# The fourth layer's support made tile by tile during the third layer, and its epilogue taken off TensorE

## What is computed

```python
h = relu(layernorm(x)); x = x + L0(h, adj, ...)      # graph attention, elu
h = relu(layernorm(x)); x = x + L1(h, adj, W, b)     # normalized adj @ h @ W + b, relu
h = relu(layernorm(x)); x = x + L2(h, adj, weight)   # adj @ (sign(h) @ sign(weight).T), relu
h = relu(layernorm(x)); x = x + L3(h, adj, t, weight)

def L3(x, adj, t, weight):
    ts = t[0]
    support = x @ weight
    return (1.0 - ts) * support + ts * (adj @ support)
```

## Time and profile before

| what | us |
|---|---|
| median of three runs | 1079.34 (1078.74 to 1080.77) |
| the profiled execution | 1078.3 |
| its span, first to last instruction | 1076.6 |
| first layer and preparation, to about | 609 |
| second layer, to about | 804.5 |
| third layer, to about | 882 |
| fourth layer, last product at about | 1058.4 |

### The profile page before, as it was taken

The page is one execution under the profiler, slowest core; times in us unless marked ns, Lnnn a source line. Parts: engine busy times, 40 slices in busy tenths (PEclk is TensorE's granted clock), DMA queues, the critical chain, the costliest instruction groups (busy, mean ns, idle before and its releaser), DMA issues.

```text
span 1076.6 us, 21117 instructions
## 1 busy us (share of the span) xinstructions
PE 998.5 (93%) x7641; PEld 749.5 (70%) x7641; DVE 754.3 (70%) x1171; ACT 540.0 (50%) x895; POOL 82.7 (8%) x114
## 2 busy tenths in 40 slices
PE   8275699999999999999999979999999999999994
PEld 8164588888888888888888735555558874555552
DVE  6778887797797797797796445555556775555552
ACT  5588887787787787787787522222220001111110
POOL 1571000000000000000012000000003330000000
PEclk8578899999999999999999989999999999999997
DMA  5022442433333333343333115555455446666660
GB/s 223 11 80 72 136 122 86 123 122 87 120 121 88 117 121 89 117 121 90 116 116 121 58 42 183 188 190 177 172 176 195 140 155 197 211 211 213 209 210 18
DMA packets 36527, 143.73 MB, mean 134 GB/s; under 512 B 4206, under 2 KB 17671, under 8 KB 36359
## 3 DMA queue, kind: packets, MB, share of 16 engines
q1 hardware_dynamic: 35255, 142.37, 40.5%
q10 hardware_dynamic: 1232, 0.85, 0.3%
HBM read 128.72 MB, written 14.50 MB: 133 GB/s over the span
## 4 chain that ended last, share of the span: by engine, by line
PE 83%; DVE 6%; issue 3%; ACT 3%; POOL 2%; DMA 1%; ACTq 0%; DVEq 0%; POOLq 0%
PE f_ya L1228 33%; PE f_ya L1153 20%; PE f_yb L1153 18%; PE f_yb L1137 8%; ACT f_gb L931 2%; POOL f_y_sb L850 1%; DVE f_s_mat L1427 1%; PE f_yb L1131 1%; PE f_ya L1131 1%; DVE f_s_mat L1422 1%; DMA f_ident<-ident_dram 1%; PE f_ya L1218 1%; ACT f_s_mat L941 1%; DVE f_wm L1418 1%; DVE f_gb L1419 1%
## 5 line engine op out<-in xcount | busy, mean ns | idle before, releaser
L1153 PE MATMUL f_ya<-f_x_mat,f_s_mat 128*128 128x257 f16 x2028 | 356.3, 275 | 33.6 <-DVE f_s_mat L1427 33.6
L1153 PE MATMUL f_yb<-f_x_mat,f_s_mat 128*128 128x257 f16 x2028 | 338.1, 276 | 0.0
L1228 PE MATMUL f_ya<-f_x_mat,f_a 128*128 128x512 f16 x1352 | 317.8, 381 | 3.5 <-DVE f_x_mat L1478 3.5
L1228 PEld LDWEIGHTS f_ya<-f_x_mat,f_a 128*128 128x128 fp8e4 x1352 | 131.5, 98 | 136.9 <-DVE f_x_mat L1478 3.9
L1153 PEld LDWEIGHTS f_yb<-f_x_mat,f_s_mat 128*128 128x128 f16 x2028 | 197.8, 98 | 30.5
L1153 PEld LDWEIGHTS f_ya<-f_x_mat,f_s_mat 128*128 128x128 f16 x2028 | 151.3, 98 | 54.1 <-issue 34.7
L931 ACT ACTIVATE f_gb<-f_e_tile,f_expc 128x256 f32<-128x256 f32 x338 | 140.4, 499 | 21.7 <-DVE f_s_mat L1427 21.7
L1422 DVE SCALAR_TENSOR_TENSOR f_s_mat<-f_wm,f_s_mat 128x1792 f16<-128x1792 f32 (+1 forms) x52 | 98.4, 1892 | 67.3 <-ACT f_s_mat L941 66.1
L1156 PE MATMUL f_ya<-f_ones,f_a 128*128 128x1 f16 x676 | 112.9, 167 | 0.0
L1418 DVE TENSOR_TENSOR f_wm<-f_gb,f_a 128x1792 f32<-128x1792 f32 (+1 forms) x52 | 98.2, 1888 | 10.5 <-ACT f_gb L931 8.8
L1536 DVE SCALAR_TENSOR_TENSOR f_gb<-f_gb 128x1664 f32<-128x1664 f32 x52 | 98.0, 1887 | 10.4 <-DVE f_s_mat L1586 10.4
(11 more groups left out here) (135 smaller groups left out, 847.0 us busy)
## 6 DMA issues: line engine op xcount, KB each, us to landing
f_gb<-adj_dram SPq DMA_DIRECT2D x52, 832.0 KB, 5.3
f_a<-f_a_dram SPq DMA_DIRECT2D x39, 832.0 KB, 4.5
f_a<-adj_t_dram SPq DMA_DIRECT2D x26, 896.0 KB, 5.0
f_a<-adj_t_dram SPq DMA_DIRECT2D x26, 768.0 KB, 4.6
f_a_dram<-f_a SPq DMA_DIRECT2D x26, 224.0 KB, 5.1
f_a_dram<-f_a SPq DMA_DIRECT2D x26, 192.0 KB, 4.6
out_dram<-f_s_mat SPq DMA_DIRECT2D x25, 128.0 KB, 4.3
f_xs<-x_dram SPq DMA_DIRECT2D x3, 768.0 KB, 8.9
```

The source lines that it names most:

```text
L1153: return pe.matmul(bank[:, 0:F + 1], s_mat[:, j, side, i], x_mat[:, j, x_side, 0:F + 1], start=start, stop=stop)
L1228: return pe.matmul(bank_a[p][:, 0:W], a8_pair[:, r, at:at + P], x_layer[layer][:, j, 0:W], start=(j == 0), stop=(j == TILES - 1))
```

## The change

The fourth layer now multiplies by the weight first. `support = h @ weight` is made tile by tile while the third layer's products run, and the adjacency product is taken on it:

- `norm` (DVE) makes centred times inverse root in one f32 step, without rectifying, into `ubuf`.
- `support_turn` (PE) transposes tile t-2 inside tile t of the third layer, ahead of block 14.
- ACT rectifies it on the way into f16 (`yt16`), and `support_low` (DVE) makes the f16 low part.
- `support_project` (PE, ahead of block 24) multiplies high x high, high x low and low x high parts with the weight, which `w3_16` holds in two f16 parts scaled by 256: six matmuls of 256 columns.
- ACT copies the f16 high part of the scaled support to `x_layer[3]`. DVE makes the low part and adds (1-t) x support to `xs` (`support`).
- In the fourth layer a tile is the 26 blocks alone; `output` (DVE) adds both halves times t to `xs` and SP stores it. `held` becomes 2 there. The supports of the last two tiles are made inside the fourth layer's first part.
- DVE makes `w3_16` in the second layer, and tests the weight's range (`w_top`, `w_far`) between the last support and the first output of the fourth layer.
- PE's first four tiles after the held part are written out ahead of the loop, in all three layers. SP stores tile t-1 after product t, where it stored t-2.

```diff
 ...
-        EPILOGUE_AT = {1: (9, 15), 3: (13, 19)}
+        EPILOGUE_AT = (9, 15)
+        SUPPORT_AT = (14, 24)
 ...
                                 load_check(q + 14, p, t + 28)
-                                store(t - 2, p)
+                                store(t - 1, 1 - p)
 ...
+                def pair2(k, first):
+                    for p in range(2):
+                        t = 2 * k + p
+                        a.wait_ge(zt_psum[3], t + 1)
+                        if not (first and p == 0):
+                            a.wait_ge(p_done[3], t)
                         settle()
+                        a.activation(yt16[:, 0, 0:F], ep[:, 0:F], ACT.Relu).then_inc(zt_done[3], 1)
+                        a.wait_ge(p_done[3], t + 1)
+                        settle()
+                        a.activation(x_layer[3][:, bass.ds(t, 1), 0:F], bank_b[p][:, 0:F].rearrange("p (a f) -> p a f", a=1),
+                                     ACT.Copy, scale=S3 / (WS * SCALE)).then_inc(x3_hi, 1)
 ...
+                def support_turn(t, p, first=False):
+                    pe.wait_ge(nrm, t + 1)
+                    if not first:
+                        pe.wait_ge(zt_low, t)
+                    settle()
+                    for c in range(FB):
+                        tr = pe.transpose(ep[:, c * P:(c + 1) * P], ubuf[:, p, c * P:(c + 1) * P], ident[:])
+                    tr.then_inc(zt_psum[3], 1)
 ...
+                def support_project(t, p, first=False):
 ...
+                    pe.wait_ge(zt_low, t + 1)
+                    if not first:
+                        pe.wait_ge(sup_added, t - 1)
+                    settle()
+                    for c in range(FB):
+                        for y_part, w_part in ((0, 0), (0, 1), (1, 0)):
+                            mm = pe.matmul(bank_b[p][:, 0:F], yt16[:, y_part, c * P:(c + 1) * P], w3_16[:, w_part, c, :],
+                                           start=(c + y_part + w_part == 0), stop=(c == FB - 1 and y_part == 1))
+                    mm.then_inc(p_done[3], 1)
 ...
+                    def output(t, p, k, first=False):
 ...
+                        v.wait_ge(mm_done[3], t + 1)
 ...
+                        v.scalar_tensor_tensor(w_res[:], bank_a[p][:, F:2 * F], t_scaled[:], xt, ALU.mult, ALU.add)\
+                         .then_inc(sum3, 1)
+                        v.wait_ge(sum3, t + 1)
+                        if not first:
+                            v.wait_ge(stored[p], 16 * k)
+                        settle()
+                        v.scalar_tensor_tensor(xo[:, p, :], bank_a[p][:, 0:F], t_scaled[:], w_res[:], ALU.mult, ALU.add)\
+                         .then_inc(z_done[3], 1)
 ...
                             if layer == 2:
+                                if last and p == 1:
+                                    norm(t - 1, 1 - p)
                                 update(t, p, k)
+                                if not (first and p == 0) and not (last and p == 1):
+                                    norm(t - 1, 1 - p)
+                                if not first:
+                                    support(t - 2, p)
                                 if not (first and p == 0):
-                                    norm(t - 1, 1 - p)
-                                continue
+                                    support_low(t - 1)
```

More of the change, by code:

```diff
@@ L34 @@
 UP, DOWN = 64.0, 2048.0
+WS, S3 = 256.0, 16.0
+W_MAX, W_MIN = 15.0, 2.0 ** -6
 GROUPS = [(g, min(4, TILES - g)) for g in range(0, TILES, 4)]
@@ L825, in _ @@
                         pair(PAIRS - 2, r0 ^ 1, False)
-                        for t in range(TILES - 4, TILES):
+                        for t in range(TILES - 3, TILES):
                             store(t, t % 2, t == TILES - 1)
@@ new lines, in turned_copy, with pair1 @@
+                def turned_copy(t):
+                    a.wait_ge(zt_psum[1], t + 1)
+                    a.activation(yt_sb[:, 0:F], ep[:, 0:F], ACT.Copy).then_inc(zt_done[1], 1)
+                def pair1(k, first):
+                    for p in range(2):
+                        t = 2 * k + p
+                        if not first:
+                            sign_product(t - 2)
+                        if not (first and p == 0):
+                            turned_copy(t - 1)
+                        product(t, p)
@@ new lines, in _ @@
+                in_pairs(a, pair1)
+                sign_product(TILES - 2)
+                turned_copy(TILES - 1)
+                sign_product(TILES - 1)
+                def pair2(k, first):
+                    for p in range(2):
+                        t = 2 * k + p
+                        a.wait_ge(zt_psum[3], t + 1)
+                        if not (first and p == 0):
+                            a.wait_ge(p_done[3], t)
+                        settle()
+                        a.activation(yt16[:, 0, 0:F], ep[:, 0:F], ACT.Relu).then_inc(zt_done[3], 1)
[3 more added lines that the diff above has]
+                                     ACT.Copy, scale=S3 / (WS * SCALE)).then_inc(x3_hi, 1)
@@ L1229, in block, with tile @@
                                          start=(j == 0), stop=(j == TILES - 1))
-                    def tile(q, p, r, n):
+                    def tile(q, p, r, n, first=False):
                         t = 2 * q + p
@@ L1277, in _ @@
                         mm.then_inc(mm_done[layer], 1)
-                    if layer != 2:
-                        layer_epilogue(layer, 0, 0, 0)
-                        layer_epilogue(layer, 0, 0, 1, True)
-                    with pe.Fori(0, PAIRS // 2) as k:
+                    if layer == 1:
+                        second_epilogue(0, 0, 0)
+                        second_epilogue(0, 0, 1, True)
+                    tile(1, 0, r0 ^ 1, 16, True)
+                    tile(1, 1, r0 ^ 1, 16)
+                    tile(2, 0, r0, 32)
+                    tile(2, 1, r0, 32)
+                    with pe.Fori(1, PAIRS // 2) as k:
                         for i in range(2):
@@ L1642, in _ @@
                         pair(PAIRS - 1, False, True)
+                    else:
+                        check(CHECKS1, 1)
+                        check(CHECKS1 + 1, 0)
+                        step = chain(flc, 3)
+                        step(v.tensor_reduce(w_top[:, 0, :], w3_16[:, 0], AX.X, ALU.max))
+                        step(v.tensor_reduce(w_top[:, 1, :], w3_16[:, 0], AX.X, ALU.min))
+                        step(v.scalar_tensor_tensor(w_top[:, 0, :], w_top[:, 1, :], -1.0, w_top[:, 0, :], ALU.mult, ALU.max))
+                        step(v.tensor_scalar(w_far[:], w_top[:, 0, :], WS * W_MAX, None, ALU.is_gt))
+                        step(v.scalar_tensor_tensor(w_far[:], w_top[:, 0, :], WS * W_MIN, w_far[:], ALU.is_lt, ALU.add))
+                        v.tensor_reduce(flags[:, 3:4], w_far[:], AX.X, ALU.add).then_inc(wflag, 1)
+                        v.wait_ge(wflag, 1)
+                        pair(0, True)
+                        with v.Fori(1, PAIRS - 1) as k:
+                            pair(k, False)
+                        pair(PAIRS - 1, False, True)
+                    if layer == 1:
+                        update(TILES - 1, 1, PAIRS - 1)
                     if layer == 2:
                         norm(TILES - 1, 1)
-                    else:
-                        if layer == 3:
-                            v.wait_ge(flagd, 2)
-                            v.tensor_scalar(general, bank_c[0:1, 0:1], NP - N + 0.5, None, ALU.is_gt).then_inc(flagd, 1)
-                        update(TILES - 1, 1, PAIRS - 1)
+                        support_low(TILES - 1)
+                        for p in range(2):
+                            support(TILES - 2 + p, p)
+                    if layer == 3:
+                        v.wait_ge(flagd, 2)
+                        v.tensor_scalar(general, bank_c[0:1, 0:1], NP - N + 0.5, None, ALU.is_gt).then_inc(flagd, 1)
 def gnn_program(nc, io):
```

172 lines of the change are left out of this document (86 added, 86 removed).

## The result

The changed kernel takes a median of **1098.84 us** (1097.33 to 1101.82, 4 runs) beside 1079.6 us (1078.74 to 1080.77, 4 runs) of the kernel before on the same chip. The ratio is **1.018, with a 95% interval of 1.016 to 1.021**: slower by 19 us. I had forecast 1085.1 us and a range up to 1092.0, so the sign was right and the size was not. The profiled execution has a span of 1096.4 us against 1076.6.

A forecast was written before the change was run, and what follows sets the result against it. PE's own work was taken to bound the third and fourth layers. The terms 36.0 + 0.6 - 26.2 - 4.6 = +5.8 us, with the median 1.0 above this execution, gave 1085.1 us, range 1077.5 to 1092.

The forecast's parts named there:

- the fourth layer's tiles: Fourth layer: the epilogue of 1.09 us goes from each of 24 tiles, leaving 5.61 us a tile: -26.2 us.
- The end: After the last product: two dependent DVE steps of 1.11 us remain in place of 5.67 us: -4.6 us.
- Between the layers: Fourth layer's first block to third tile: 15.9 us for 15.3, PE standing still 2.9 us for DVE's queue: +0.6 us.
- rival 2: The 2.9 us standstill between the layers lowers the clock; PE loses 4 us, 1089 us in all; chance 0.12.
- The second layer: Two added DVE steps of about 0.6 us each, hidden ahead of a DVE wait of 4.47 us: nothing.
- The third layer's tiles: Third layer: a loop through four engines sets 4.34 us a tile in place of 2.84, over 24 tiles: +36.0 us.
- DVE to PE: Third layer's loop, hop from DVE's norm to PE's transposes: 0.06 us, plus 0.02 for two waits on some tiles.
- transposes to ACT 0.48: Third layer's loop, hop from PE's transposes to ACT's rectified copy: 0.48 us.
- The break-even at 4.10 us a tile: The third layer's tile time at which the whole change would neither gain nor lose: 4.10 us.
- Rival 1: Third layer's loop is hidden and PE's own work sets 3.71 us a tile: -9.3 us, 1070.0 us; chance 0.14.
- Rivals 4 and 5: Clock sinks through whole third layer, about 1158 us, chance 0.03; weights' range check sends kernel into general program, given nothing.
- Rival 3: Transfers bound the fourth layer: 6.5 us a tile, only 5 us given back, 1106 us; chance 0.05.

The follow-up runs named there:

- the written-out kernel: The changed kernel with the third layer's loops on PE, DVE and ACT written out with constant tile numbers, small semaphore steps kept: 1091.82 us.
- the kernel without the small steps: The changed kernel with seven small semaphore instructions between wait and work left out on PE, ACT and DVE: 1088.03 us, 1088.02 in a second profile.

## Right and wrong, step by step

- **What bounds the kernel before, and the fourth layer's tiles**: right. 5.61 us a tile without a gap, -26.2 us, the clock at 1.00. That DVE has over 2 us of slack for the stores held only just: it waited for them 13 times, up to 3.1 us at once, and in the written-out kernel, with the same fourth layer, one such wait stopped PE.
- **The end**: right, -4.85 for -4.6. From the start of the first output step to the end of the second it is 1.14 us (1083.23 to 1084.37), for 1.11 forecast.
- **Between the layers**: right in what PE waits for, +0.2 for +0.6; the standstill was 2.22 us and not 2.9. The two reductions cost 0.71 from start to start for an estimated 0.85, the tiny steps 0.20 for 0.31. The clock did not fall, so rival 2 did not come about here, but it did in three other kernels, at 1.7 us and not the 4 that I had put on it.
- **The second layer**: right, 204.9 us before and after, and six steps more were hidden as well (204.9 with them, in the kernel with the supports later).
- **The third layer's tiles**: right in the mechanism, in its two waits, in who ends them and in the products' price; wrong in size. The step that failed is the length of the loop, 4.34 for 4.88, and in it the hops "DVE to PE" (0.56 for 0.43 from the norm's start, in it the norm's own 0.41 for 0.35), "transposes to ACT 0.48" (0.56), the 0.13 ahead of the norm (0.26) and "PE to DVE" (1.18 for 1.08 from the products' start). I took the first two from rows of before whose instructions follow their wait at once, while the new ones have a semaphore step between, and put nothing for the register work. The two overheads cost 0.69 us a tile together (4.88 to 4.19); the miss is only 0.54, mostly because the two hops round the low part had been put 0.09 too long each, which is luck. My range of 4.2 to 4.6 was made of long and short ends of the same kind of row, so it held none of this. At 24 tiles x 0.54 that is 13.0 us. With 1.7 of the start, and 0.4 and 0.3 less than forecast between the layers and at the end, it gives the miss of 14.0 us in the span.
- **The break-even at 4.10 us a tile**: close. At 4.19 a tile the rest of the span is 263.7 us against 262.6, which puts it at 4.14.
- **Rival 1** was not what the change did, but it is what the kernel with the supports a tile later does: priced at 1070.0, measured at 1070.74. **Rivals 4 and 5** are false: the granted clock was 1.00 in the whole third layer, and nothing of the general program runs.
- **Rival 3**: false. The fourth layer moved 242 GB/s. But stores took a median of 5.9 us to land against 4.3 before, and in three other kernels that reached PE.
- **The rule on micro-idles** (the Trainium skill, TensorE: Matmul & The Clock Gate, "A second HAM failure mode: psum-queue depth-cycling"): two idles of 0.2 to 0.6 us in every tile of 4.88 for 116 us left the granted clock at 1.00, so here the trace does not agree.

## What to carry to other kernels

When work is added to a tile, follow its inputs back to the last matmul of the tile before: if they get there, the period is the sum of the loop, whatever the engines' busy shares, and one more tile of distance turned a loss of 1.8% into a gain of 0.8% here. Price every hop of such a loop from a row whose instruction waits in the same way, with the same extra instructions between wait and work and the same register arithmetic; a tenth of a microsecond at each of five hops would be 12 us over 24 tiles. When a wait is shortened, look behind it before the gain is booked: here a store and then the clock took it back.

## What the runs showed of the hardware

- A semaphore increment as an instruction of its own between a wait and its work made the hop 0.09 to 0.10 us longer on PE, ACT and DVE (0.08 to 0.13 where the loop was written out). In the third layer with a tile of slack it cost nothing (88.2 us with and without).
- Wait values and addresses made from a loop's register, with the loop's branch, cost 0.25 us a tile on a loop through three engines (4.88 to 4.63), and this adds to the cost above.
- After a PE standstill of about 2 us the granted clock fell to 0.50 for about 3.4 us in three kernels (in one of them in both of its profiles), 0.4 to 1.3 us after PE had started again, and stayed at 1.00 after standstills of the same length in others.
- The part ahead of the third layer's third tile took from 813.67 to 817.06 us in these profiles, a spread as large as several of the effects above; only the rest of the span could tell them apart. The second layer's part was 204.8 to 204.9 us in ten of the fourteen profiles and 206.0 to 206.1 in four, and the kernel without the small steps, profiled twice, had 204.8 once and 206.0 once.
